# Draining a projection from two PSUM banks instead of four, with the square and the column sums cut in halves

## The chip, the cores and the metric

The kernel runs on one Trainium2 chip, the same program on all 8 cores. Each core has two of the 16 sequences, and no core waits for another. The time is device microseconds of the slowest core: 2117.3 us as the median of 9 runs (2113.49 to 2324.63). The profile is of one execution on core 0.

Four engines matter here. TensorE (PE) multiplies and writes to PSUM, eight banks of 128x512 float32, called `pb[0]` to `pb[7]`. VectorE (DVE) does the element-wise work and reads the banks. ScalarE (ACT) does Ln, Exp and ReLU. DMA queues move the weights and the tiles; GpSimd (POOL) and SyncE (SP) only issue DMAs. Each engine runs its own instructions in program order, and engines wait for each other by counting semaphores: `s_T` counts what PE has done, `s_V` DVE, `s_S` ACT.

## The reference

One layer on x of 16 sequences x 2048 positions x 1024 features:

```
x = x + attn(layernorm(x))      # attn is a linear recurrence (a scan), not softmax
x = x + ffn(layernorm(x))

attn(x): delta = 0.99*sigmoid(x @ W_t.T + b_t) + 0.01
         Bu    = x @ W_b.T + b_b                    # 16 states
         h     = scan over positions: h = exp(A*delta)*h + Bu
         y     = (h @ W_c.T + b_c) + x * D
         return y @ W_o.T + b_o                     # 1024 x 1024
ffn(x):  h = bitlinear(x, w_fc) + gate*(x @ v.T @ fast_b.T @ u.T)    # 1024 -> 4096
         return bitlinear(relu(h)**2, w_proj)                        # 4096 -> 1024
layernorm(x) = (x - mean) / sqrt(mean(x*x) - mean**2 + 1e-5)
bitlinear rounds a weight matrix to -1, 0, 1 times a scale.
```

## The kernel before

Features lie on partitions and positions on the free axis. A tile is 512 positions x 1024 features, held as 8 column blocks of 128 features (`DCH = 8`); a core has 8 tiles, j = 0 to 7. A first stage of some 400 us rounds the weights and writes them to scratch memory. Then the tiles go through a pipeline written out by hand:

```
    for i in range(nt):
        emit_ffnA(i)
        rs1 = emit_front1(i + 2) if i + 2 < nt else None
        emit_ffnB(i)
        if i + 1 < nt:
            s2 = emit_back1(i + 1)
        if i + 2 < nt:
            emit_front1b(i + 2, rs1, ffb_last[i])
        if i + 1 < nt:
            emit_back2(i + 1, s2)
        if i + 2 < nt:
            emit_front2(i + 2)
```

Each `emit_` call appends instructions to the engines' queues in this order, so the order of the calls is the order on every engine. Tile 0 goes through `front1`, `front1b`, `front2`, `back1` and `back2` ahead of the loop, and tile 1 through the three front parts.

- `emit_ffnA` (L898): 256 matmuls in 32 groups of 8 that alternate between banks 2 and 3; ACT drains each group with a ReLU (L919) and DVE squares the result (L929).
- `emit_front1` (L552 to L605): square, cast and column sums of the tile two ahead, and its layer-norm statistics.
- `emit_ffnB` (L954): 256 matmuls, alternating between banks 6 and 7; DVE adds each group to the residual (L972).
- `emit_back1` (L723 to L801): the recurrence's output (L723 and L748), then the 1024 x 1024 projection with W_o, called `_wo` here: 64 matmuls (L768), 8 for each of 8 column blocks. Block `oc` goes to bank `2 + oc % 4`. DVE drains four blocks after the fourth is done, adding the bias `bo_s` and the input `x_s` (L782, in `_wo_stt`); PE may start the second four after all four banks are drained. After the eighth drain DVE squares the whole tile (L799) and casts it to bf16 (L801).
- `emit_front1b` (L619 to L632): the first layer norm of the tile two ahead, on DVE: two groups of 8 instructions that write `tls` and `xnb`.
- `emit_back2` (L812 to L877): the second layer norm. `_stats2` on PE sums the columns of the cast (L812, bank 0) and of the square (L815, bank 1) by 8 matmuls each with a matrix of ones; DVE reads the sums at L823 and L825, ACT does Ln and Exp, and DVE writes the normalised tile (L867, L877).
- `emit_front2` (L645 to L706): the projection to 2 x 16 rows and the scan, with DVE and ACT handing over to each other (L656 to L706).

The next `emit_ffnA` needs the tile of `emit_back2` and, since ACT works in order, its ReLUs stand behind the Exp of `emit_front2` (L691).

Of the kernel before, what the change touches and what calls it, by code (L numbers as in the profile page):

```python
# [26 lines left out]
def build_nc(spc=SEQ_PER_CORE, tps=TILES_PER_SEQ, h=H):  # L27
# [483 lines left out]
    def _gx2(g):  # L511
# [22 lines left out]
    ffa_last = {}  # L534
    sq_chunks = {}
    ffb_last = {}
    run = {"statsv1": 0, "wo_stt": 0, "final": 0, "yb": 0, "tmp2": 0,
           "tls": 0, "nz": 0, "relu": 0}
# [171 lines left out]
    def emit_back1(j):  # L710
# [48 lines left out]

        def _wo(te, j=j, V1=V1):  # L760
            wait(te, "tensor", "s_V", yb_done[j])
            wait(te, "tensor", "s_S", run["relu"])
            for oc in range(DCH):
                b = 2 + oc % 4
                if oc >= 4:
                    wait(te, "tensor", "s_V", V1 + 1)
# [6 lines left out]

        def _wo_stt(ve, j=j):
            if j >= 2:
                wait(ve, "vector", "s_out%d" % (j % 2), 16 * ((j - 2) // 2 + 1))
            for g in range(2):
                wait(ve, "vector", "s_T", wod[4 * g + 3])
                last = None
                for q in range(4):  # L780
                    oc = 4 * g + q
                    last = ve.scalar_tensor_tensor(out=xn32[:, p, oc], in0=pb[2 + oc % 4][:],  # L782
                                                   scalar=bo_s[:, oc:oc + 1],
                                                   in1=x_s[:, p, oc],
                                                   op0=ALU.add, op1=ALU.add)
                inc(last, "s_V")
# [10 lines left out]
        def _sqln2(ve, j=j, ws=ws):  # L797
            wait(ve, "vector", "s_V", ws)
            ve.tensor_tensor(out=xnb[:, p], in0=xn32[:, p], in1=xn32[:, p],  # L799
                             op=ALU.mult)  # L800
            inc(ve.tensor_copy(out=yb[:], in_=xn32[:, p]), "s_V")  # L801
        blk.vector(_sqln2)
        return ctr["s_V"]

    def emit_back2(j, sq2_done):
        p = j % 2

        def _stats2(te, j=j, sq2_done=sq2_done):
            wait(te, "tensor", "s_V", sq2_done)
            wait(te, "tensor", "s_V", yb_done[j])  # L810
            for dc in range(DCH):
                te.matmul(pb[0][:], ones_b[:], yb[:, dc],  # L812
                          start=(dc == 0), stop=(dc == DCH - 1))
            for dc in range(DCH):
                i2 = te.matmul(pb[1][:], ones_b[:], xnb[:, p, dc],  # L815
# [67 lines left out]
    def emit_ffnA(i):  # L883
# [37 lines left out]
        run["relu"] = ctr["s_S"]  # L921
# [181 lines left out]
```

How the kernel before makes its waits and increments, by code:

```python
    def inc(ins, name, k=1):  # L167
        ins.then_inc(sems[name], k)
        ctr[name] += k
        return ctr[name]
# [1 line left out]
    def wait(e, ename, name, val):  # L172
        if val is None or val <= 0:
            return
        key = (ename, name)
        if lastwait.get(key, 0) >= val:
            return
        e.wait_ge(sems[name], val)
        lastwait[key] = val
```

## Time and profile before

| | |
|---|---|
| median of 9 runs | 2117.3 us |
| the profiled execution | 2117.43 us, of which its span is 2115.9 us |
| cores | 2100.4 to 2115.9 us |
| PE busy | 1390.7 us (66%) |
| DVE busy | 891.9 us (42%) |
| ACT busy | 332.5 us (16%) |
| granted TensorE clock, mean over the span | 0.82 of full speed |

No engine is busy all the time. The shares are averages over stages of different kinds: within a tile, PE works almost without a gap in the two feed-forward stages, and between them DVE and ACT work through a long chain while PE mostly waits. So a stage has to be read by its own timeline. A matmul's row is longer (379 ns) than the distance between two of them, because matmuls overlap.

### The profile page before, as it was taken

To read this page: it belongs to the slowest core of one execution; us is meant where nothing else is said; L and a number is where in the kernel's file an instruction comes from. 1 tells how busy PE (TensorE), PEld (TensorE's weight loads), DVE (VectorE), ACT (ScalarE), POOL (GpSimd) and SP (SyncE) were. 2 spreads that over 40 slices of the span, in tenths; PEclk is the share of its full clock that TensorE was granted. 3 is DMA by queue.
4 is the path that set the end of the run, shared out by engine and by line. 5 is a ranking of instruction groups with operands and counts; after the bars stand their busy time and mean duration, and the time that the engine had idled before them with its cause. 6 is when DMAs were issued, how large, how long until landed. Compare 5 with 4: busy or idle time off the path is not lost.

```text
span 2115.9 us, 14743 instructions; the slowest of 8 cores (2100.4 to 2115.9 us)
## 1 busy us (share of the span) xinstructions
PE 1390.7 (66%) x5768; PEld 620.5 (29%) x5768; DVE 891.9 (42%) x925; ACT 332.5 (16%) x392; POOL 27.0 (1%) x42
## 2 busy tenths in 40 slices
PE   1444354324288739874896589568956885798498
PEld 0111154301133314321342234223422332343143
DVE  1777878554612271236214521543164325312410
ACT  1111112010131013002300220032003200310120
POOL 0000000000000000000000000000000000000000
PEclk9766577657699979986998799779978997898799
DMA  6333446421031413241334024312521250234033
GB/s 124 99 119 119 119 139 186 154 97 40 0 120 67 172 40 120 81 158 44 115 106 172 23 97 154 124 43 77 183 96 62 77 214 5 81 118 159 20 120 139
DMA packets 73236, 221.43 MB, mean 105 GB/s; under 512 B 4512, under 2 KB 37280, under 8 KB 54720
## 3 DMA queue, kind: packets, MB, share of 16 engines
q1 hardware_dynamic: 60208, 167.79, 23.4%
q0 software_dynamic: 12960, 52.69, 7.0%
q8 instruction: 47, 0.77, 0.2%
q14 instruction: 21, 0.17, 0.0%
HBM read 189.28 MB, written 33.55 MB: 105 GB/s over the span
## 4 chain that ended last, share of the span: by engine, by line
PE 57%; DVE 28%; issue 6%; ACT 4%; DMA 4%; DVEq 0%; POOL 0%; POOLq 0%; ACTq 0%; SPq 0%
PE pb L954 21%; PE pb L898 20%; PE pb L768 6%; PE pb L357 3%; DVE xn L782 2%; PE pb L442 2%; DVE tls L622 2%; DVE tls L867 2%; DVE xnb L632 2%; DVE xnb L877 2%; DVE cb L383 2%; DVE sqbuf L552 2%; DVE cb L384 2%; DMA woT_b<-woT 2%; DMA wsl<-wprojT 1%
## 5 line engine op out<-in xcount | busy, mean ns | idle before, releaser
L898 PE MATMUL pb<-xnb,wcmb_st 128*128 128x512 bf16 x2048 | 468.5, 393 | 134.8 <-DVE but L658 79.2
L954 PE MATMUL pb<-r2b,wproj_st 128*128 128x512 bf16 x2048 | 444.0, 379 | 0.6 <-DMA wproj_st<-wproj_sc 0.5
L898 PEld LDWEIGHTS pb<-xnb,wcmb_st 128*128 128x128 bf16 x2048 | 205.0, 101 | 398.4 <-issue 174.3
L954 PEld LDWEIGHTS pb<-r2b,wproj_st 128*128 128x128 bf16 x2048 | 199.9, 98 | 243.3 <-issue 3.9
L929 DVE TENSOR_TENSOR r2b<-r2b 128x4096 bf16<-128x4096 bf16 x32 | 73.4, 2292 | 385.3 <-ACT r2b L919 385.3
L972 DVE TENSOR_TENSOR xn<-xn,pb 128x512 f32<-128x512 f32 x64 | 44.0, 688 | 366.3 <-PE pb L954 366.3
L919 ACT ACTIVATE r2b<-pb 128x512 bf16<-128x512 f32 x256 | 152.1, 597 | 286.7 <-PE pb L898 286.6
L768 PE MATMUL pb<-yb,woT_b 128*128 128x512 bf16 x512 | 130.8, 420 | 37.1 <-DVE xn L782 23.8
L844 ACT ACT_TABLE_LOAD x8 | 10.3, 1283 | 762.4 <-DVE statB L838 762.4
L560 PE MATMUL pb<-xb,ones_b 128*128 128x512 bf16 x64 | 28.6, 626 | 125.1 <-DVE xb L553 125.1
L782 DVE SCALAR_TENSOR_TENSOR xn<-pb,bo_s,x_s 128x512 f32<-128x512 f32 x64 | 43.6, 745 | 135.6 <-PE pb L768 135.6
L304 PE MATMUL pb<-GTb,v_b 16*128 16x512 bf16 x64 | 22.1, 450 | 115.3 <-DVE wr L311 115.2
L768 PEld LDWEIGHTS pb<-yb,woT_b 128*128 128x128 bf16 x512 | 53.1, 106 | 118.1 <-issue 71.7
L812 PE MATMUL pb<-yb,ones_b 128*128 128x512 bf16 x64 | 28.2, 619 | 77.7 <-DVE yb L801 77.7
L645 PE MATMUL pb<-xnb,wbtT_b 128*16 128x512 bf16 x64 | 28.6, 626 | 61.5 <-DVE xnb L632 61.5
L442 PE MATMUL pb<-aw32p,ones 128*128 128x128 f32 x256 | 39.7, 332 | 42.3 <-ACT aw32p L434 42.3
L723 PE MATMUL pb<-hbt,wcT_b 16*128 16x512 bf16 x64 | 26.8, 511 | 60.9 <-DVE yb L748 48.8
L442 PEld LDWEIGHTS pb<-aw32p,ones 128*128 128x128 f32 x256 | 39.0, 247 | 43.7 <-issue 43.7
L560 PEld LDWEIGHTS pb<-xb,ones_b 128*128 128x128 bf16 x64 | 8.2, 138 | 141.8 <-issue 141.8
L748 DVE SCALAR_TENSOR_TENSOR yb<-pb,bc_s,tmp 128x512 bf16<-128x512 f32 x64 | 45.1, 746 | 5.5 <-PE pb L723 2.9
L304 PEld LDWEIGHTS pb<-GTb,v_b 16*128 16x128 bf16 x64 | 5.7, 99 | 133.1 <-issue 129.6
L552 DVE TENSOR_TENSOR sqbuf<-x_s 128x4096 bf16<-128x4096 f32 x8 | 35.3, 4418 | 19.6 <-DMA x_s<-xT 19.6
(106 smaller groups left out, 1153.8 us busy)
## 6 DMA issues: line engine op xcount, KB each, us to landing
wcmb_st<-wcmb_sc SPq DMA_DIRECT2D x64, 1024.0 KB, 4.8
wproj_st<-wproj_sc SPq DMA_DIRECT2D x64, 1024.0 KB, 5.0
x_s<-xT POOLq DMA_DIRECT2D x8, 2048.0 KB, 8.4
yT<-xn POOLq DMA_DIRECT2D x8, 2048.0 KB, 9.2
wsl<-wfcT SPq DMA_DIRECT2D x4, 2048.0 KB, 10.3
wslB<-wfcT SPq DMA_DIRECT2D x4, 2048.0 KB, 10.2
wcmb_sc<-wr POOLq DMA_DIRECT2D x8, 1024.0 KB, 4.1
wsl<-wprojT SPq DMA_DIRECT2D x4, 2048.0 KB, 9.7
```

The lines of the kernel that those rows point to most:

```text
L357: i2 = te.matmul(pb[0][:], ones32[:], av[:, dc], start=(dc == 0), stop=(dc == DCH - 1))
L383: ve.tensor_tensor(out=cb1[:], in0=wv[:], in1=hf, op=ALU.is_gt)
L442: i2 = te.matmul(pb[0][:, 0:128], ones32[:], av2[:, kc], start=(kc == 0), stop=(kc == hch - 1))
L552: ve.tensor_tensor(out=sqbuf[:], in0=src, in1=src, op=ALU.mult)
L748: ins = ve.scalar_tensor_tensor(out=yb[:, dc], in0=pb[dc % 2][:], scalar=bc_s[:, dc:dc + 1], in1=tmp2[:, q], op0=ALU.add, op1=ALU.add)
L768: i2 = te.matmul(pb[b][:], woT_b[:, kc, oc * 128:(oc + 1) * 128], yb[:, kc], start=(kc == 0), stop=(kc == DCH - 1))
L782: last = ve.scalar_tensor_tensor(out=xn32[:, p, oc], in0=pb[2 + oc % 4][:], scalar=bo_s[:, oc:oc + 1], in1=x_s[:, p, oc], op0=ALU.add, op1 ...
L898: i2 = te.matmul(pb[b][:], wcmb_st[:, hs % 2, dc, (hc % 4) * 128:(hc % 4 + 1) * 128], xnb[:, p, dc], start=(dc == 0), stop=(dc == DCH - 1))
L919: inc(sc.activation(out=r2b[:, hc], in_=pb[b][:], func=AF.Relu), "s_S")
L929: inc(ve.tensor_tensor(out=r2b[:, qq * QS:(qq + 1) * QS], in0=r2b[:, qq * QS:(qq + 1) * QS], in1=r2b[:, qq * QS:(qq + 1) * QS], op=ALU.mul ...
L954: i2 = te.matmul(pb[b][:], wproj_st[:, oc % 2, kc, :], r2b[:, kc], start=(kc == 0), stop=(kc == hch - 1))
L972: inc(ve.tensor_tensor(out=xn32[:, p, oc], in0=xn32[:, p, oc], in1=pb[b][:], op=ALU.add), "s_V")
```

## The change

`_wo` now uses two banks, 4 and 5, alternating by block, and each drain signals for itself: PE may start block `oc` as soon as block `oc - 2` is drained. DVE waits for each block by itself and drains it at once. The numbers in `STTN` are the counts of `s_V`: the fifth count is the first half of the square, so that blocks 4 to 7 have the counts 6 to 9. The wait of `_wo` for the ReLUs (`run["relu"]`) goes with banks 2 and 3.

The square of the tile is cut in two: the first four blocks are squared right behind the fourth drain, the last four behind the eighth; the cast follows. `_stats2` sums the square first, in two halves with a wait each, and then the cast; it uses banks 7 and 6 in place of 1 and 0. The load of the tile two ahead (`_pref`) waits for the count behind the cast rather than the one behind the last drain.

```diff
@@ emit_back1
+        STTN = [1, 2, 3, 4, 6, 7, 8, 9]
+
         def _wo(te, j=j, V1=V1):
             wait(te, "tensor", "s_V", yb_done[j])
-            wait(te, "tensor", "s_S", run["relu"])
             for oc in range(DCH):
-                b = 2 + oc % 4
-                if oc >= 4:
-                    wait(te, "tensor", "s_V", V1 + 1)
+                b = 4 + oc % 2
+                if oc >= 2:
+                    wait(te, "tensor", "s_V", V1 + STTN[oc - 2])
                 for kc in range(DCH):
                     i2 = te.matmul(pb[b][:], woT_b[:, kc, oc * 128:(oc + 1) * 128],
                                    yb[:, kc], start=(kc == 0), stop=(kc == DCH - 1))
@@ _wo_stt
-            for g in range(2):
-                wait(ve, "vector", "s_T", wod[4 * g + 3])
-                last = None
+            for g2 in range(2):
                 for q in range(4):
-                    oc = 4 * g + q
-                    last = ve.scalar_tensor_tensor(out=xn32[:, p, oc], in0=pb[2 + oc % 4][:],
-                                                   scalar=bo_s[:, oc:oc + 1],
-                                                   in1=x_s[:, p, oc],
-                                                   op0=ALU.add, op1=ALU.add)
-                inc(last, "s_V")
+                    oc = 4 * g2 + q
+                    b = 4 + oc % 2
+                    wait(ve, "vector", "s_T", wod[oc])
+                    inc(ve.scalar_tensor_tensor(out=xn32[:, p, oc], in0=pb[b][:],
+                                                scalar=bo_s[:, oc:oc + 1],
+                                                in1=x_s[:, p, oc],
+                                                op0=ALU.add, op1=ALU.add), "s_V")
+                hw = ctr["s_V"]
+
+                def _sqh(ve2, j=j, g2=g2, hw=hw):
+                    wait(ve2, "vector", "s_V", hw)
+                    sl = slice(4 * g2, 4 * g2 + 4)
+                    inc(ve2.tensor_tensor(out=xnb[:, p, sl], in0=xn32[:, p, sl],
+                                          in1=xn32[:, p, sl], op=ALU.mult), "s_V")
+                _sqh(ve)
+                sqh[g2] = ctr["s_V"]
+            inc(ve.tensor_copy(out=yb[:], in_=xn32[:, p]), "s_V")
+            sqh[2] = ctr["s_V"]
-        def _sqln2(ve, j=j, ws=ws):
-            wait(ve, "vector", "s_V", ws)
-            ve.tensor_tensor(out=xnb[:, p], in0=xn32[:, p], in1=xn32[:, p],
-                             op=ALU.mult)
-            inc(ve.tensor_copy(out=yb[:], in_=xn32[:, p]), "s_V")
-        blk.vector(_sqln2)
@@ emit_back2
-            wait(te, "tensor", "s_V", sq2_done)
-            wait(te, "tensor", "s_V", yb_done[j])
+            wait(te, "tensor", "s_V", back1_sqh[j][0])
+            wait(te, "tensor", "s_V", run["final"])
+            for dc in range(4):
+                te.matmul(pb[7][:], ones_b[:], xnb[:, p, dc],
+                          start=(dc == 0), stop=False)
+            wait(te, "tensor", "s_V", back1_sqh[j][1])
+            for dc in range(4, DCH):
+                te.matmul(pb[7][:], ones_b[:], xnb[:, p, dc],
+                          start=False, stop=(dc == DCH - 1))
+            wait(te, "tensor", "s_V", back1_sqh[j][2])
             for dc in range(DCH):
-                te.matmul(pb[0][:], ones_b[:], yb[:, dc],
-                          start=(dc == 0), stop=(dc == DCH - 1))
-            for dc in range(DCH):
-                i2 = te.matmul(pb[1][:], ones_b[:], xnb[:, p, dc],
+                i2 = te.matmul(pb[6][:], ones_b[:], yb[:, dc],
                                start=(dc == 0), stop=(dc == DCH - 1))
```

The first place is DVE's queue around the drains, for a tile in the loop. In the names, `xn_44` is `xn32`, the residual; `pb` is any bank; `[waits s_T]` says that the instruction waits for PE. Before:

```order
L782 SCALAR_TENSOR_TENSOR xn_44<-pb,bo_s,x_s 128x512 [waits s_T]
L782 SCALAR_TENSOR_TENSOR xn_44<-pb,bo_s,x_s 128x512 x3
L782 SCALAR_TENSOR_TENSOR xn_44<-pb,bo_s,x_s 128x512 [waits s_T]
L782 SCALAR_TENSOR_TENSOR xn_44<-pb,bo_s,x_s 128x512 x3
L802 UNCONDITIONAL_BRANCH
L799 TENSOR_TENSOR xnb<-xn_44 128x4096 [waits s_V]
L801 CAST yb<-xn_44 128x4096
```

The same place of DVE's queue in the changed kernel, whose line numbers differ:

```order
L786 SCALAR_TENSOR_TENSOR xn_44<-pb,bo_s,x_s 128x512 [waits s_T] x4
L795 TENSOR_TENSOR xnb<-xn_44 128x2048 [waits s_V]
L786 SCALAR_TENSOR_TENSOR xn_44<-pb,bo_s,x_s 128x512 [waits s_T] x4
L795 TENSOR_TENSOR xnb<-xn_44 128x2048 [waits s_V]
L799 CAST yb<-xn_44 128x4096
```

Half of the square has moved ahead of the fifth drain, and each drain waits for its own block.

The second place is PE's queue from the projection to the sums, for the first tile; `yb` is first the projection's input and later the cast, `woT_b` the projection's weight, `ones_b` the matrix of ones. Before:

```order
L768 MATMUL pb<-yb,woT_b 128x512 [waits s_V]
L768 MATMUL pb<-yb,woT_b 128x512 x31
L768 MATMUL pb<-yb,woT_b 128x512 [waits s_V]
L768 MATMUL pb<-yb,woT_b 128x512 x31
...
L812 MATMUL pb<-yb,ones_b 128x512 [waits s_V]
L812 MATMUL pb<-yb,ones_b 128x512 x7
L815 MATMUL pb<-xnb,ones_b 128x512 x8
```

The end of the projection (its last block) and the sums in PE's queue of the changed kernel:

```order
L770 MATMUL pb<-yb,woT_b 128x512 [waits s_V]
L770 MATMUL pb<-yb,woT_b 128x512 x7
L832 UNCONDITIONAL_BRANCH
L821 MATMUL pb<-xnb,ones_b 128x512 x4
L825 MATMUL pb<-xnb,ones_b 128x512 [waits s_V]
L825 MATMUL pb<-xnb,ones_b 128x512 x3
L829 MATMUL pb<-yb,ones_b 128x512 [waits s_V]
L829 MATMUL pb<-yb,ones_b 128x512 x7
```

The projection has a wait in front of each block from the third on instead of one in the middle, and the sums of the square have moved ahead of those of the cast, with the only wait for the whole cast in front of the last 8.

## Rows read from the trace of the kernel before

**Rows 1.** The page: span, and shares of the chain that ended last.

```profile
span 2115.9 us, 14743 instructions; the slowest of 8 cores (2100.4 to 2115.9 us)
...
PE 57%; DVE 28%; issue 6%; ACT 4%; DMA 4%; DVEq 0%; POOL 0%; POOLq 0%; ACTq 0%; SPq 0%
```

**Rows 2.** Groups by line: line, engine, shapes, count | busy us, mean ns | idle.

```profile
L768 PE MATMUL pb<-yb,woT_b 128*128 128x512 bf16 x512 | 130.8, 420 | 37.1 <-DVE xn L782 23.8 <-DVE yb L748 13.3
L782 DVE SCALAR_TENSOR_TENSOR xn<-pb,bo_s,x_s 128x512 f32<-128x512 f32 x64 | 43.6, 745 | 135.6 <-PE pb L768 135.6
...
L632 DVE TENSOR_TENSOR xnb<-tls,statA 128x512 bf16<-128x512 f32 x64 | 39.2, 684 | 0.8
...
L799 DVE TENSOR_TENSOR xnb<-xn 128x4096 bf16<-128x4096 f32 x8 | 35.4, 4425 | 0.8
```

**Rows 3.** Waits: who waited for whom: total us, times, longest us.

```profile
PE pb L768 <- DVE xn L782: 23.8, 8, 3.0
...
DVE statB L823 <- PE pb L815: 13.0, 2, 6.6
```

**Rows 4.** Timeline of one tile: start us, us, instruction, count [idle before].

```profile
1108.97 0.90 SPq L987 DMA_DIRECT2D wcmb_st<-wcmb_sc  x2
...
1133.48 9.09 PE L768 MATMUL pb<-yb,woT_b 128*128 128x512 bf16 x32 [1.68 <-DVE yb L748]
1133.86 0.15 PEld L768 LDWEIGHTS pb<-yb,woT_b 128*128 128x128 bf16 x1 [0.27 <-issue]
1134.29 0.15 PEld L768 LDWEIGHTS pb<-yb,woT_b 128*128 128x128 bf16 x1 [0.28 <-issue]
...
1142.68 2.73 DVE L782 SCALAR_TENSOR_TENSOR xn<-pb,bo_s,x_s 128x512 f32<-128x512 f32 x4 [9.45 <-PE pb L768]
...
1145.55 7.07 PE L768 MATMUL pb<-yb,woT_b 128*128 128x512 bf16 x32 [2.98 <-DVE xn L782]
1152.72 2.73 DVE L782 SCALAR_TENSOR_TENSOR xn<-pb,bo_s,x_s 128x512 f32<-128x512 f32 x4 [7.32 <-PE pb L768]
1155.56 4.42 DVE L799 TENSOR_TENSOR xnb<-xn 128x4096 bf16<-128x4096 f32 x1
1156.01 0.88 POOL L793 DMA_DIRECT2D x_s<-xT  x1 [31.06 <-DVE xn L782]
1159.90 2.29 DVE L801 CAST yb<-xn 128x4096 bf16<-128x4096 f32 x1
1162.10 0.68 DVE L619 TENSOR_TENSOR statA<-statA 128x512 f32<-128x512 f32 x1
...
1162.33 3.57 PE L812 MATMUL pb<-yb,ones_b 128*128 128x512 bf16 x8 [9.71 <-DVE yb L801]
...
1172.53 0.68 DVE L823 TENSOR_SCALAR statB<-pb 128x512 f32<-128x512 f32 x1
...
1192.11 5.34 PE L898 MATMUL pb<-xnb,wcmb_st 128*128 128x512 bf16 x16 [12.89 <-DVE but L658]
...
1201.78 1.09 ACT L919 ACTIVATE r2b<-pb 128x512 bf16<-128x512 f32 x2
...
1202.52 12.81 PE L898 MATMUL pb<-xnb,wcmb_st 128*128 128x512 bf16 x51 [5.07 <-ACT r2b L919]
```

**Rows 5.** Windows: stretch, its us, busy us (count) by engine, PEclk, DMA.

```profile
1127.40:1137.60 10.20, 6.13 (x14) 1.73 (x15) 5.27 (x10) 0.00 (x0) 0.00 (x0) 0.50 0.45 186
1137.60:1154.60 17.00, 12.04 (x55) 5.12 (x53) 4.60 (x7) 0.00 (x0) 0.00 (x0) 1.00 0.00 0
...
1202.50:1205.80 3.30, 3.28 (x8) 1.19 (x9) 0.00 (x0) 0.36 (x1) 0.00 (x0) 0.50 0.02 5
1206.00:1256.00 50.00, 50.00 (x233) 22.50 (x230) 6.88 (x3) 17.32 (x29) 0.00 (x0) 1.00 0.35 126
```

**Rows 6.** Timeline of the last tile, around its sums.

```profile
1950.45 8.50 PE L768 MATMUL pb<-yb,woT_b 128*128 128x512 bf16 x32 [2.98 <-DVE xn L782]
...
1968.67 3.57 PE L812 MATMUL pb<-yb,ones_b 128*128 128x512 bf16 x8 [9.71 <-DVE yb L801]
...
1974.95 0.69 DVE L823 TENSOR_SCALAR statB<-pb 128x512 f32<-128x512 f32 x1 [6.42 <-PE pb L815]
```

More of the change, by code:

```diff
@@ L534, in build_nc @@
     ffa_last = {}
+    back1_sqh = {}
     sq_chunks = {}
@@ L537, in build_nc @@
     run = {"statsv1": 0, "wo_stt": 0, "final": 0, "yb": 0, "tmp2": 0,
-           "tls": 0, "nz": 0, "relu": 0}
+           "tls": 0, "nz": 0}
     def emit_front1(j):
@@ L772, in emit_back1 @@
         wo_mm[j] = dict(wod)
+        sqh = {}
         def _wo_stt(ve, j=j):
@@ L795, in emit_back1 @@
             blk.gpsimd(_pref)
-        def _sqln2(ve, j=j, ws=ws):
-            wait(ve, "vector", "s_V", ws)
-            ve.tensor_tensor(out=xnb[:, p], in0=xn32[:, p], in1=xn32[:, p],
-                             op=ALU.mult)
-            inc(ve.tensor_copy(out=yb[:], in_=xn32[:, p]), "s_V")
-        blk.vector(_sqln2)
+        back1_sqh[j] = dict(sqh)
         return ctr["s_V"]
@@ L822, in _sv2 @@
             wait(ve, "vector", "s_T", st)
-            ve.tensor_scalar(out=mB, in0=pb[0][:], scalar1=1.0 / D,
+            ve.tensor_scalar(out=mB, in0=pb[6][:], scalar1=1.0 / D,
                              scalar2=None, op0=ALU.mult)
-            inc(ve.tensor_scalar(out=uB, in0=pb[1][:], scalar1=1.0 / D,
+            inc(ve.tensor_scalar(out=uB, in0=pb[7][:], scalar1=1.0 / D,
                                  scalar2=EPS, op0=ALU.mult, op1=ALU.add), "s_V")
@@ L920, in emit_ffnA @@
         blk.scalar(_relu)
-        run["relu"] = ctr["s_S"]
         QS = max(1, hch // 4)
```

## The prediction

> **What bounds the kernel now.** I read the page first, for the span and the chain that ended last [rows 1]: PE has 57% of the chain and DVE 28%, so stages that PE bounds alternate with stages that DVE bounds, and the shares alone do not say which kind the change touches. The groups by line [rows 2] then give a duration and a count for each instruction concerned: 64 drains of 0.745 us (L782) and 8 squares of 4.425 us (L799) in 8 tiles. The waits [rows 3] name two that the change touches: PE waits 8 times for the drains, 23.8 us in all, and DVE waits twice for the column sums, 13.0 us in all. Last comes the timeline of one tile in the loop [rows 4], where the reader is to follow who waits for whom. PE does 32 matmuls of the projection (1133.48, 9.09 us); DVE drains four blocks (1142.68, 2.73 us) while PE stands still for 2.98 us; PE does 32 more (7.07 us); DVE drains four more, squares (4.42 us), casts (2.29 us) and goes at once into the next layer norm (1162.10). From there to the first ReLU (1201.78) and to the restart of PE's long stage (1202.52) the work is DVE's and ACT's, in a chain in which the drains' end sets the start of everything. So every microsecond by which the cast ends earlier moves the restart by as much, unless something else is late. The weights of the restart are no candidate: their loads were issued at 1108.97, 93 us ahead of it [rows 4].
>
> **Part 1: PE's wait in the middle of the projection.** It is 2.98 us in each of the 8 tiles [rows 3, 4]. With two banks in turn, PE starts block 2 when block 0 is drained. A block is a quarter of 7.07 us, 1.77 us, at the full clock; the way from a block's end through its drain back to PE is 0.11 (1142.57 to 1142.68) + 0.745 + 0.14 (1145.41, the end of the drains, to 1145.55) = 1.0 us [rows 2, 4]. That lies beside the other bank's block, so blocks 2 to 5 start without a wait. Block 6 waits for the drain of block 4, and the half square now stands in front of that drain in DVE's queue. No row has a half square. Two float32 products of two tensors bound it, 0.684 us for 512 columns (L632) and 4.425 us for 4096 [rows 2]: the slope is 3.741 / 3584 = 1.044 ns per column, so 2048 columns take 0.684 + 1536 x 0.001044 = 2.29 us. From the end of block 3: 0.11 + 0.745 + 0.11 + 2.29 + 0.745 + 0.14 = 4.14 us until PE may start block 6. PE has blocks 4 and 5 to do, 3.53 us. So it stands still for 0.6 us. From below the stall is 0 (if DVE's instructions overlap a little more), from above 2.3 us (the half square wholly exposed); I take 0.6, the sum of the rows. Gain of the part: 2.98 - 0.6 = 2.4 us per tile.
>
> **Part 2: the drains after the last block.** Before, four stand there, 2.73 us; now one, 0.745 us, as the other three lie beside PE's blocks. Gain 2.0 us per tile. The waits of each drain for its own block cost nothing: behind them in DVE's queue stands only the rest of the same tile.
>
> **Part 3: the square.** After the last drain 4.42 us become 2.29 us; the first half lies beside PE's blocks 4 and 5, and what it costs there is the stall of part 1. Gain 2.1 us per tile. The cast stays at 2.29 us.
>
> **Part 4: the column sums.** In six tiles the layer norm of another tile stands between the cast and the read of the sums on DVE, from 1162.10 to 1172.53, 10.4 us; PE's 16 sums take less (13.0 us of waiting in 2 tiles is all there is), so their order and banks are worth nothing there [rows 3, 4]. In tiles 0 and 7 nothing stands between, and DVE waits 6.6 and 6.4 us [rows 3, 6]. There 8 of the 16 sums now lie ahead of the end of the cast: four start right behind the projection, four behind the second half square, beside the 2.29 us of the cast. Left are 8. At 1.2 GHz 8 take 3.57 us (L812 [rows 4, 6]), with 0.25 us of handing over 3.8 us; at 2.4 GHz, a quarter of 7.07 us and the same, 2.0 us. PE has worked with shorter pauses before them than before, so either is possible; I take the middle, 2.9 us. Gain 3.6 us in each of two tiles, 7.2 us together (bounds 5.4 and 9.0).
>
> **What costs nothing.** The wait for the ReLUs that goes was never the last one: PE starts the projection on DVE's `yb` (L748), 1.68 us after its own last work [rows 4]. The load of the tile two ahead waits for the cast now; the cast ends where the last drain ended before (1155.5 against 1155.45), so the load is issued at the time it was (1156.01). PE's first four sums wait for counts that the projection has waited for already.
>
> **The sum.** Parts 1 to 3 give 2.4 + 2.0 + 2.1 = 6.5 us in each of 8 tiles, 52 us; part 4 gives 7 us; together 59 us. The profiled execution took 2117.43 us (span 2115.9, 1.5 us around it), which is the median of the runs within 0.2 us: 2117.4 - 59 = 2058.4 us.
>
> **The clock.** TensorE was granted 0.50 (1.2 GHz) until 1137.60, that is for the first ten matmuls of the projection (4.12 us at 0.43 us each), after a stretch in which it had little to do, and 1.00 (2.4 GHz) from there to the end of the second group, over its own pause of 2.98 us too [rows 5]. At 1.2 GHz two weight loads are 0.43 us apart (1133.86, 1134.29), at 2.4 GHz a matmul takes 7.07 / 32 = 0.22 us: 0.21 us for each that changes sides. With shorter pauses I keep the ten at 1.2 GHz and expect the rest at 2.4. After the wait of 5.07 us the restart has 8 matmuls at 1.2 GHz [rows 4, 5]; the stretch ahead of it is the same chain as before, so I keep these 8 too.
>
> A rule of the Trainium skill speaks against this part of the change: "TensorE: Matmul & The Clock Gate", section "A second HAM failure mode: psum-queue depth-cycling", tells of a kernel that goes round its PSUM banks, pauses briefly between groups, and swings between both clocks. By that rule the projection with two banks would lose what rival 3 below loses. This case's trace disagrees as far as it goes: the long stage L898 alternates between two banks as well and was granted 1.00 for 50 us [rows 5].
>
> **Rivals.**
>
> 1. *The gain is partly given back.* Either the half square holds PE up for its whole 2.3 us, 1.7 us more than taken in 8 tiles: 2072 us; or the restart, coming at another moment, has 16 matmuls at 1.2 GHz in place of 8: 8 x 0.21 = 1.7 us in 7 tiles, 2070 us. For it: DVE's queue is strict, and the last tile had a second group of 8.50 us instead of 7.07 [rows 6], so the clock does not fall at the same matmul each time. Against it: PE's wait is the same in all 8 tiles (23.8 us, the longest 3.0 [rows 3]), so the tiles repeat each other closely. Chance 10%.
>
> 2. *More is gained.* If the restart has no matmuls at 1.2 GHz, 7 tiles give another 12 us: 2046 us. Against it: PE still stands for 5 us before it. Chance 6%.
>
> 3. *Slower: two banks keep the projection at 1.2 GHz.* The place is the projection; the price is 64 matmuls at 0.43 us, 27.5 us, against 9.09 + 2.98 + 7.07 = 19.1 us, so 8.4 us more per tile in place of part 1's gain. Parts 2 and 3 still give 4.1, so the tile loses 4.3 us, 8 tiles 34 us, less 7 us of part 4: 2144 us. It decides when the lost matmuls outweigh 6.5 + 0.9 us per tile: 7.4 / 0.21 = 35 more than the ten, 45 of the 64. Against it: one wait of 0.6 us in a stretch that kept the clock over 2.98 us. Chance 2%.
>
> 4. *Nothing moves.* If something other than DVE's chain held the ReLU or the restart, the saved time would stand there as a new wait, and the time stays at 2117 us. I find no such thing in the timeline: the weights are there, and DVE has no idle time in front of L619 or L823 [rows 4]. Chance 2%.
>
> **How the numbers follow.** The forecast, 2058 us, has 80%; its own range, by the bounds of the stall (5 us down) and of the sums and half of a clock effect, is 2051 to 2066. The rivals have 10, 6, 2 and 2%. For 8 in 10 the range reaches somewhat towards rivals 1 and 2: 2047 to 2069. A difference of 0.2% (4 us) is about what a measurement of this kernel can tell from none. Faster takes the forecast and rivals 1 and 2, 96%; the same is rival 4, 2%; slower rival 3, 2%.
>
> **What would show it.** In the changed kernel's timeline the projection is one burst of about 16.8 us with at most one pause, of about 0.6 us, in front of block 6; behind it stand one drain, a square of 2.29 us and the cast; from the projection's start to the cast's end it takes about 22.2 us rather than 28.7. In the list of waits the 23.8 us of PE for the drains fall to about 5, DVE's wait for PE at the drains goes from 16 waits to many short ones, and the two waits for the sums fall from 6.5 to about 3 us. The distance from one tile's projection to the next falls by 6.5 us. Wrong would be: a pause before other blocks (the drains are slower than taken), a projection at clock 0.50 beyond the first dozen matmuls (rival 3), more matmuls at 1.2 GHz at the restart (rival 1), or a new idle time in front of L619 or the first ReLU (rival 4).

## The result, and the profile after

The changed kernel takes 2057.04 us as the median of 10 runs (2053.77 to 2241.16), the kernel before 2118.3 us beside it; the ratio is 0.971, with a 95% interval of 0.9702 to 0.9719. The forecast was 2058, the saving forecast 59 us; measured it is 61. (The highest times come from runs in which one die ran at a lower clock; the ratios leave them out.)

The page of the kernel after, profiled on core 1; it answers to [rows 1].

```profile
span 2057.0 us, 14848 instructions; the slowest of 8 cores (2040.9 to 2057.0 us)
...
PE 57%; DVE 29%; issue 6%; ACT 4%; DMA 4%; DVEq 0%; POOL 0%; POOLq 0%; ACTq 0%; SPq 0%
```

The shares are those of before within one point: 59 us of span went, and the page alone would not tell from where. The groups by line do (busy us, mean ns of one, idle before). L770 is the projection, L786 the drain, L795 the new half square; they answer to [rows 2].

```profile
L770 PE MATMUL pb<-yb,woT_b 128*128 128x512 bf16 x512 | 128.8, 415 | 17.7 <-DVE yb L749 12.9 <-DVE xn L786 4.9
L786 DVE SCALAR_TENSOR_TENSOR xn<-pb,bo_s,x_s 128x512 f32<-128x512 f32 x64 | 47.3, 749 | 75.9 <-PE pb L770 75.9
L795 DVE TENSOR_TENSOR xnb<-xn 128x2048 bf16<-128x2048 f32 x16 | 36.7, 2292 | 1.7
```

A drain costs what it did (749 ns after 745), and two half squares cost 36.7 us in all after 35.4 for the whole ones. So no instruction became cheaper; what fell is waiting. The waits (total us, times, longest us) answer to [rows 3]:

```profile
DVE xn L786 <- PE pb L770: 75.9, 48, 3.8
...
DVE statB L837 <- PE pb L829: 6.7, 2, 3.8
...
PE pb L770 <- DVE xn L786: 4.9, 8, 0.6
```

PE's waits for the drains are still 8, but of 0.6 us instead of 3.0. DVE waits 48 times for a block, 1.6 us each, 75.9 us in all, where it waited for whole groups of four before, 135.6 us in all [rows 2]. The timeline of one tile on core 1 (start us, us, instruction, count [idle before]) answers to [rows 4]:

```profile
1112.62 12.25 PE L770 MATMUL pb<-yb,woT_b 128*128 128x512 bf16 x48 [1.56 <-DVE yb L749]
...
1121.53 0.75 DVE L786 SCALAR_TENSOR_TENSOR xn<-pb,bo_s,x_s 128x512 f32<-128x512 f32 x1 [0.97 <-PE pb L770]
1122.38 2.29 DVE L795 TENSOR_TENSOR xnb<-xn 128x2048 bf16<-128x2048 f32 x1
1124.59 1.40 DVE L786 SCALAR_TENSOR_TENSOR xn<-pb,bo_s,x_s 128x512 f32<-128x512 f32 x2
...
1125.48 3.61 PE L770 MATMUL pb<-yb,woT_b 128*128 128x512 bf16 x16 [0.61 <-DVE xn L786]
...
1129.20 0.75 DVE L786 SCALAR_TENSOR_TENSOR xn<-pb,bo_s,x_s 128x512 f32<-128x512 f32 x1 [0.97 <-PE pb L770]
1130.05 2.29 DVE L795 TENSOR_TENSOR xnb<-xn 128x2048 bf16<-128x2048 f32 x1
1132.26 2.29 DVE L799 CAST yb<-xn 128x4096 bf16<-128x4096 f32 x1
...
1164.48 5.02 PE L912 MATMUL pb<-xnb,wcmb_st 128*128 128x512 bf16 x16 [13.21 <-DVE but L659]
...
1174.89 10.33 PE L912 MATMUL pb<-xnb,wcmb_st 128*128 128x512 bf16 x41 [5.39 <-ACT r2b L933]
```

Six blocks run without a pause, the one pause stands in front of block 6, and behind the last block come one drain, a half square and the cast, which ends at 1134.55: 21.9 us after the projection's start, where it was 28.7. PE's restart at 1174.89 is 62.3 us after that start; in [rows 4] it is 69.0. The 6.8 us by which the cast came earlier arrive whole at the restart. The windows of the same tile (stretch, its us, busy us (count) of PE, PEld, DVE, ACT and POOL, PEclk, DMA) answer to [rows 5]:

```profile
1112.60:1116.30 3.70, 3.68 (x10) 1.32 (x11) 0.00 (x0) 0.00 (x0) 0.00 (x0) 0.52 0.00 0
1116.30:1129.10 12.80, 12.19 (x57) 5.41 (x56) 7.37 (x8) 0.00 (x0) 0.00 (x0) 1.00 0.00 0
1174.80:1178.20 3.40, 3.31 (x10) 1.29 (x11) 0.00 (x0) 0.44 (x2) 0.00 (x0) 0.59 0.00 0
1178.40:1228.40 50.00, 49.77 (x231) 22.37 (x229) 6.88 (x3) 17.24 (x30) 0.00 (x0) 1.00 0.35 126
```

Again some ten matmuls at the start of the projection are at 1.2 GHz, the rest at 2.4, over the pause of 0.61 us too; and at the restart again about 3 us are at 1.2 GHz.

### The profile page after: what moved, and what is told of

Read it like the earlier page. It is cut to its first block, busy times and chain, and to the rows that moved or that the text cites. A ratio compares the mean times of both kernels' runs of the same rounds, so it can differ in the third digit from the quotient of the medians.

```text
span 2057.0 us, 14848 instructions; the slowest of 8 cores (2040.9 to 2057.0 us)
## 1 busy us (share of the span) xinstructions
PE 1375.6 (67%) x5768; PEld 614.2 (30%) x5768; DVE 896.1 (44%) x933; ACT 332.6 (16%) x392; POOL 26.9 (1%) x42
## 4 chain that ended last, share of the span: by engine, by line
PE 57%; DVE 29%; issue 6%; ACT 4%; DMA 4%; DVEq 0%; POOL 0%; POOLq 0%; ACTq 0%; SPq 0%
PE pb L912 21%; PE pb L967 21%; PE pb L770 5%; PE pb L357 3%; PE pb L442 2%; DVE tls L881 2%; DVE tls L623 2%; DVE xnb L633 2%; DVE xnb L891 2%; DVE cb L383 2%; DVE sqbuf L553 2%; DVE cb L384 2%; DMA woT_b<-woT 2%; DVE cb L471 2%; DVE cb L472 1%
## 5 line engine op out<-in xcount | busy, mean ns | idle before, releaser
L912 PE MATMUL pb<-xnb,wcmb_st 128*128 128x512 bf16 x2048 | 466.9, 392 | 137.8 <-DVE but L659 81.5
L912 PEld LDWEIGHTS pb<-xnb,wcmb_st 128*128 128x128 bf16 x2048 | 204.5, 100 | 400.2 <-issue 175.4
L770 PE MATMUL pb<-yb,woT_b 128*128 128x512 bf16 x512 | 128.8, 415 | 17.7 <-DVE yb L749 12.9
L770 PEld LDWEIGHTS pb<-yb,woT_b 128*128 128x128 bf16 x512 | 52.6, 105 | 97.2 <-issue 49.8
L786 DVE SCALAR_TENSOR_TENSOR xn<-pb,bo_s,x_s 128x512 f32<-128x512 f32 x64 | 47.3, 749 | 75.9 <-PE pb L770 75.9
L442 PE MATMUL pb<-aw32p,ones 128*128 128x128 f32 x256 | 39.7, 332 | 46.1 <-DVE dbuf L478 18.6
```

The lines of the kernel that those rows point to most:

```text
L442: i2 = te.matmul(pb[0][:, 0:128], ones32[:], av2[:, kc], start=(kc == 0), stop=(kc == hch - 1))
L770: i2 = te.matmul(pb[b][:], woT_b[:, kc, oc * 128:(oc + 1) * 128], yb[:, kc], start=(kc == 0), stop=(kc == DCH - 1))
L786: inc(ve.scalar_tensor_tensor(out=xn32[:, p, oc], in0=pb[b][:], scalar=bo_s[:, oc:oc + 1], in1=x_s[:, p, oc], op0=ALU.add, op1=ALU.add), " ...
L912: i2 = te.matmul(pb[b][:], wcmb_st[:, hs % 2, dc, (hc % 4) * 128:(hc % 4 + 1) * 128], xnb[:, p, dc], start=(dc == 0), stop=(dc == DCH - 1))
```

## The experiments

Three theories were held against each other; the expectations name them by letters. A: the saving is a sum of microseconds on the chain from the projection through DVE to PE's restart, as predicted. B: the same, but what reaches the time depends on how many matmuls run at 1.2 GHz after it. C: the saving is TensorE's clock, which shorter pauses keep up.

To hold the kernels against each other, this table has the means over the five inner tiles (1 to 5) of all 8 cores (40 distances), read out of the traces: from a projection's start to the end of the cast and to PE's restart (us), the us at granted clock 0.50 within the projection and behind the restart, and the distance from one projection's start to the next.

```
kernel       cast end  restart  1.2 GHz: projection  restart   distance
before         28.62    68.95            3.96         3.27      204.83
x1_drains      23.80    64.21            4.55         5.20      201.27
x2_halves      27.78    68.12            6.53         4.97      204.75
x3_sums        28.59    68.93            3.90         3.24      204.77
after          22.15    62.48            3.97         3.26      198.10
x4_fourbanks   21.43    61.77            4.08         3.41      197.99
x5_quarters    20.51    60.99            4.37         4.82      197.93
x7_tail1       22.75    63.15            3.96         5.24      199.66
x7_tail4       24.46    64.87            4.19         3.99      201.38
x8_front4      22.25    62.66            4.03         3.64      198.42
x10_fill       22.02    62.39            3.82         0.00      196.32
x6_ahead       20.34    55.14            4.03         3.38      191.23
x12_allfill    18.71    53.53            0.70         0.00      185.48
```

### The parts one by one

**Drains and banks alone** (x1_drains), on the kernel before; the square stays whole, the sums stay behind the cast.

```diff
-                b = 2 + oc % 4
-                if oc >= 4:
-                    wait(te, "tensor", "s_V", V1 + 1)
+                b = 4 + oc % 2
+                if oc >= 2:
+                    wait(te, "tensor", "s_V", V1 + oc - 1)
...
-            for g in range(2):
-                wait(ve, "vector", "s_T", wod[4 * g + 3])
+            for oc in range(DCH):
+                wait(ve, "vector", "s_T", wod[oc])
```

> The kernel before with two banks and a drain of its own for each block; the square stays whole and the sums stay as they were. Theory A (each part is worth what it takes off the path from the projection's start to the cast's end): 2.98 us of PE's wait and 2.0 us of drains go in each of 8 tiles, and no half square stands in front of block 4's drain, so 5.0 x 8 = 40 us: 2078 us against 2118. Theory C (the gain is TensorE's clock, since the projection has no pause any more): nearly all of the 60 us, 2060 us.

Measured: 2081.83 us, ratio 0.9826 [0.9812, 0.9839]. The groups of this kernel show that PE's pause for the drains is gone; only the wait for `yb` is left:

```profile
L767 PE MATMUL pb<-yb,woT_b 128*128 128x512 bf16 x512 | 128.8, 418 | 12.5 <-DVE yb L748 12.5
```

That is 38 us less than the kernel before beside it (2119.65). By C the whole gain, some 60 us, should have been here: C falls. The cast ends 4.8 us earlier, close to A's 5.0 (the pause of 2.98 and three drains), but the distance of the tiles falls by 3.6 only: behind the restart 5.20 us are at 1.2 GHz instead of 3.27.

**The square in halves alone** (x2_halves), on the kernel before, with four banks and drains in fours.

```diff
+                wait(ve, "vector", "s_V", ctr["s_V"])
+                sl = slice(4 * g, 4 * g + 4)
+                inc(ve.tensor_tensor(out=xnb[:, p, sl], in0=xn32[:, p, sl],
+                                     in1=xn32[:, p, sl], op=ALU.mult), "s_V")
...
-            ve.tensor_tensor(out=xnb[:, p], in0=xn32[:, p], in1=xn32[:, p],
-                             op=ALU.mult)
```

> The kernel before with its four banks and its drains in fours, with the square alone cut in two halves, one behind each four drains. Theory A: 4.42 - 2.29 = 2.1 us in each of 8 tiles, 17 us: 2101 us, and PE's wait of 2.98 us stays. Theory B (TensorE's clock takes back part of a small gain at the restart of the long stage, as more matmuls at 1.2 GHz): 8 to 14 us, 2104 to 2110 us. Theory C: no change, 2118 us.

Measured: 2113.93 us, ratio 0.9972 [0.9962, 0.9981]: 6 us where the sum asks for 17. The windows of core 4 over two successive projections show why; the first four rows are one projection, the last two the next (PEclk is the third number from the end).

```profile
926.60:931.20 4.60, 4.54 (x11) 1.61 (x12) 0.00 (x0) 0.00 (x0) 0.00 (x0) 0.50 0.02 4
931.30:938.00 6.70, 4.68 (x22) 1.93 (x20) 1.91 (x3) 0.00 (x0) 0.00 (x0) 1.00 0.00 0
938.10:944.90 6.80, 5.94 (x15) 2.05 (x16) 3.01 (x3) 0.00 (x0) 0.00 (x0) 0.50 0.00 0
945.00:949.00 4.00, 3.96 (x19) 1.58 (x17) 0.00 (x0) 0.00 (x0) 0.00 (x0) 1.00 0.00 0
1132.90:1136.00 3.10, 3.03 (x8) 1.10 (x9) 0.00 (x0) 0.00 (x0) 0.00 (x0) 0.50 0.00 0
1136.10:1151.70 15.60, 12.52 (x58) 5.32 (x55) 5.02 (x5) 0.00 (x0) 0.00 (x0) 1.00 0.00 0
```

In the first projection the clock came up, fell at 938.1 in PE's pause of 2.98 us, and came up once more: 15 more matmuls ran at 1.2 GHz. In the next one it stayed up over the same pause. On this core long projections (22.2 us, 11.4 of them at 1.2 GHz) and short ones (18.6 us) alternate tile by tile. Behind the last block the half square saves 2.1 us, as A has it; the clock takes it back in the projection (6.53 us at 1.2 GHz instead of 3.96) and at the restart (4.97 instead of 3.27). That is B's side, and more of it than B had expected. What decides which projection is long stays open.

**The sums alone** (x3_sums), on the kernel before: PE takes the columns' sums of the square, which is there first, ahead of those of the cast.

```diff
+            wait(te, "tensor", "s_V", sq_only[j])
+            for dc in range(DCH):
+                te.matmul(pb[1][:], ones_b[:], xnb[:, p, dc],
+                          start=(dc == 0), stop=(dc == DCH - 1))
             wait(te, "tensor", "s_V", sq2_done)
-            wait(te, "tensor", "s_V", yb_done[j])
             for dc in range(DCH):
-                te.matmul(pb[0][:], ones_b[:], yb[:, dc],
-                          start=(dc == 0), stop=(dc == DCH - 1))
-            for dc in range(DCH):
-                i2 = te.matmul(pb[1][:], ones_b[:], xnb[:, p, dc],
+                i2 = te.matmul(pb[0][:], ones_b[:], yb[:, dc],
...
```

> The kernel before with one thing changed: the column sums take the square first, behind a wait for the square alone, and the cast after it. Theory A: only tiles 0 and 7 see it, where 8 of the 16 sums now lie beside the 2.3 us of the cast; they run at 1.2 GHz (3.4 us for 8), so 2.0 to 2.3 us are hidden in each: the two waits for the sums fall from 6.5 to 4.3 us, the time by 4 us, 2114 us against 2118. That the sums matter in the other tiles: 8 x 2 = 16 us.

Measured: 2110.56 us, ratio 0.997 [0.9958, 0.9983], so 0.3%, 6 to 7 us. Its waits give 5.7 us of that in the first and the last tile, 13.0 us before and now

```profile
DVE statB L824 <- PE pb L816: 7.3, 2, 3.7
```

and nothing in the tiles between (distance 204.77 after 204.83). A had 4 us. In the first and the last tile this order alone brings nearly all of what the whole change brings there (13.0 to 6.7 us). The three edits alone give 38 + 6 + 7 = 51 us, the whole change gives 61: the parts don't add up. Both that lie in the inner tiles gave part of their saving back to the clock, and the whole change did not.

### Two banks or four, and a finer split

**Four banks** (x4_fourbanks), on the kernel after: PE waits for the drain four blocks back, and for the ReLUs again.

```diff
-                b = 4 + oc % 2
-                if oc >= 2:
-                    wait(te, "tensor", "s_V", V1 + STTN[oc - 2])
+                b = 2 + oc % 4
+                if oc >= 4:
+                    wait(te, "tensor", "s_V", V1 + STTN[oc - 4])
...
```

> The changed kernel with four banks in turn (2 to 5) instead of two, all else as changed: block 6 waits for block 2's drain, so the half square no longer holds PE up. Theory A: the pause of 0.61 us goes in 8 tiles, 5 us: 2052 us against 2057. Theory B: the projection ends 0.6 us earlier, but the distance from tile to tile stays at 198.0 us, since the restart has more matmuls at 1.2 GHz: 2056 to 2057 us. That two banks as such matter: slower or faster than 2057 by more than 5 us.

Measured: 2057.54 us, ratio 0.9705 [0.969, 0.972]: the same. The pause of 0.6 us is gone and the cast ends 0.7 us earlier, but the tiles follow at 197.99 us. Of the 0.7 us, 0.1 go in 0.15 us more at 1.2 GHz behind the restart, and 0.4 in the 16 column sums of `emit_front1`, between the two long stages: 5.18 us of them are at 1.2 GHz in place of 4.45 (means of the same 40 tiles), and a microsecond at 1.2 GHz does half of what it does at 2.4. B had 2056 to 2057 us, for the restart alone. So the two banks were not the cost, and the stall of part 1 was not worth removing.

**The square in quarters** (x5_quarters), on the kernel after, each quarter behind two drains; 6 sums stand ahead of the last quarter.

```diff
-            for g2 in range(2):
-                for q in range(4):
-                    oc = 4 * g2 + q
+            for g2 in range(4):
+                for q in range(2):
+                    oc = 2 * g2 + q
...
```

> The changed kernel with the square in quarters, one behind every second drain. A quarter takes 0.684 + 512 x 0.001044 = 1.22 us. Theory A: behind the last drain 1.22 us instead of 2.29, and no pause in front of block 6: 1.07 + 0.61 = 1.7 us in 8 tiles, 13 us: 2044 us against 2057. Theory B: the distance from tile to tile stays at 198.0 us and only tile 0 and the stretch behind the last projection gain: 3 us, 2054 us.

Measured: 2052.32 us, ratio 0.9688 [0.9673, 0.9704]. Timeline of one tile on core 2, the last quarter, the cast and the restart; then the windows of that restart:

```profile
926.96 1.23 DVE L795 TENSOR_TENSOR xnb<-xn 128x1024 bf16<-128x1024 f32 x1
928.10 2.29 DVE L799 CAST yb<-xn 128x4096 bf16<-128x4096 f32 x1
...
971.08 4.42 PE L912 MATMUL pb<-xnb,wcmb_st 128*128 128x512 bf16 x10 [4.49 <-ACT r2b L933]
```

```profile
971.00:975.65 4.65, 4.57 (x11) 1.61 (x12) 0.00 (x0) 1.02 (x2) 0.00 (x0) 0.50 0.00 0
975.80:1010.00 34.20, 34.20 (x161) 15.48 (x159) 4.58 (x2) 11.54 (x20) 0.00 (x0) 1.00 0.43 154
```

A quarter takes 1.23 us, and the cast ends 20.5 us after the start, 1.6 earlier, as A has it. Then the restart stays at 1.2 GHz for 4.6 us (mean 4.82, after 3.26), and the tiles follow at 197.93 us. Of the 13 us that A saw in the 8 tiles 5 arrive, hardly any of them in the inner tiles (0.17 us each). The restart comes 1.5 us earlier; 0.8 of that goes behind the restart and 0.6 in the 16 column sums of `emit_front1` (5.57 us at 1.2 GHz in place of 4.45). B was nearer.

### Cost put in at the same place

**A square of 512 columns in front of the cast** (x7_tail1), on the kernel after; it writes to a buffer that nobody reads then.

```diff
+            ve.tensor_tensor(out=xb[:, 0:1], in0=xn32[:, p, 0:1],
+                             in1=xn32[:, p, 0:1], op=ALU.mult)
```

> The changed kernel with one DVE instruction more per tile, ahead of the cast: it squares 512 columns into a buffer that nobody reads at that time. Theory A (each us on the way from the drains to the cast's end is a us of the tile): 0.62 to 0.68 us in 8 tiles, 5 us: 2062 us against 2057. Theory B (the tile distance holds at a value, and TensorE's matmuls at 1.2 GHz make up the difference): the distance stays 198.0 us in the loop, only tile 0 and the stretch behind the last projection pay: 2058 us.

Measured: 2069.38 us, ratio 0.9794 [0.9753, 0.9834] (wide, as one of the times compared was 2090). The cast ends 0.60 us later, and 8 x 0.6 would make 5 us; it cost 12. Windows of core 3, the restarts of two successive tiles, each with the stretch behind it:

```profile
978.95:981.65 2.70, 2.68 (x7) 1.00 (x8) 0.00 (x0) 0.36 (x1) 0.00 (x0) 0.51 0.00 0
981.80:1000.00 18.20, 18.20 (x86) 8.29 (x85) 2.29 (x1) 6.46 (x11) 0.00 (x0) 1.00 0.37 126
1177.55:1183.10 5.55, 5.50 (x14) 1.95 (x15) 0.00 (x0) 0.99 (x2) 0.00 (x0) 0.51 0.00 0
1183.20:1200.00 16.80, 16.80 (x80) 7.64 (x78) 2.29 (x1) 5.88 (x10) 0.00 (x0) 1.00 0.34 127
```

Seven matmuls at 1.2 GHz in the one tile, fourteen in the other. The first of the two tiles is 198.57 us long, 0.5 more than the mean of the kernel after, as A has it; the other is 201.01. A (2062) and B (2058, the cost swallowed) were both too low: the clock did decide, but against this edit.

**The same with 2048 columns** (x7_tail4), 2.28 us.

```diff
+            ve.tensor_tensor(out=xb[:, 0:4], in0=xn32[:, p, 0:4],
+                             in1=xn32[:, p, 0:4], op=ALU.mult)
```

> The same with 2048 columns, 2.2 to 2.3 us per tile, as long as the half square that the change takes off this place. Theory A: 18 us, 2075 us, and the distance from tile to tile is 200.2 us. Theory B: the distance jumps from 198.0 to the next value seen so far, 201.3 us, as in the kernel with two banks alone: about 25 us, 2082 us.

Measured: 2081.78 us, ratio 0.9831 [0.9818, 0.9845]: 24 us more than the kernel of the next run, for 8 x 2.3 = 18. The cast ends 2.31 us later and the distance grows by 3.28, with 3.99 us at 1.2 GHz behind the restart in place of 3.26, and 5.13 in the column sums of `emit_front1` in place of 4.45. B had 2082. On cores 0 and 1 the long stage also has stretches at a third granted clock, here on core 0:

```profile
1396.85:1401.52 4.67, 4.67 (x20) 1.96 (x18) 2.29 (x1) 1.19 (x2) 0.00 (x0) 0.81 0.51 172
```

They are not what the edit cost: on core 5, which has none, the distance grows as much (198.00 to 201.36).

**The same square in front of the first drain** (x8_front4), where DVE waits for PE anyway: the same work, at another place.

```diff
+            ve.tensor_tensor(out=xb[:, 0:4], in0=x_s[:, p, 0:4],
+                             in1=x_s[:, p, 0:4], op=ALU.mult)
```

> The changed kernel with the same 2.3 us of DVE work per tile, put in front of the first drain, where DVE waits 3.8 us for PE's first block. Theories A and B: it is hidden, 2057 us. That DVE's busy time as such counts: 18 us, 2075 us.

Measured: 2058.05 us, ratio 0.9721 [0.9708, 0.9735]: free. Timeline of DVE on core 0:

```profile
910.04 2.28 DVE L781 TENSOR_TENSOR xb<-x_s 128x2048 bf16<-128x2048 f32 x1
913.95 0.75 DVE L788 SCALAR_TENSOR_TENSOR xn<-pb,bo_s,x_s 128x512 f32<-128x512 f32 x1 [1.63 <-PE pb L770]
```

DVE still waits 1.63 us behind it. So 2.3 us of DVE in each tile cost 24 us behind the last drain and nothing ahead of the first: the place decides, not the busy time. That is what makes parts 2 and 3 of the prediction a gain at all, since they only move DVE's work from the one place to the other.

### The clock by itself

**Twenty idle matmuls in front of the restart** (x10_fill), on the kernel after: PE does them while it waits for the first ReLU, into a bank that is not read.

```diff
+                if hc == 2 and i + 1 < nt:
+                    for _ in range(20):
+                        te.matmul(pb[0][:], ones_b[:], xnb[:, p, 0], start=True, stop=True)
```

> The changed kernel with 20 idle matmuls (into bank 0, which nobody reads then) behind the first 16 of the long stage, in the 5.4 us in which PE waits for the first ReLU; 20 take 4.3 us at 2.4 GHz. They are to keep TensorE's clock up, so that the restart has no matmuls at 1.2 GHz. Theory A: the 3.0 us at 1.2 GHz at the restart become 1.5, 7 tiles: 10 us, 2046 us. Theory B: the restart can no longer make up differences, and the distance falls to another value below 198.0, by more than the 1.5 us: up to 24 us, 2033 us. If the fillers run at 1.2 GHz they take 8.5 us and hold the restart up by 3 us: 2078 us.

Measured: 2047.95 us, ratio 0.9673 [0.9659, 0.9686]. Timeline of PE on core 1, and the window of the restart:

```profile
967.82 4.48 PE L910 MATMUL pb<-xnb,ones_b 128*128 128x512 bf16 x20
973.46 26.71 PE L915 MATMUL pb<-xnb,wcmb_st 128*128 128x512 bf16 x123 [1.16 <-ACT r2b L936]
```

```profile
973.40:1000.00 26.60, 26.54 (x123) 12.04 (x124) 3.70 (x2) 9.15 (x16) 0.00 (x0) 1.00 0.36 126
```

The restart comes at the same moment (62.39 after 62.48 us), but at 2.4 GHz from its first matmul. The 3.26 us at 1.2 GHz become 0, half of that is 1.6 us, and the tile is 1.8 us shorter; 9 us in all, near A's 2046. Nothing was computed faster ahead of it: this is the clock alone, and it is what the tested change left untouched.

**DVE's free time used** (x6_ahead). A version that takes the first half of the next tile's layer norm (nine DVE instructions) into DVE's wait ahead of the first drain, with four banks and the square in quarters:

```diff
+        md = ahead() if ahead else None
...
-            emit_front1b(i + 2, rs1, ffb_last[i])
+            emit_front1b_s(i + 2, md)
```

> The kernel with the square in quarters, with four banks for the projection, and with the first half of the next layer norm (9 instructions, 5.4 us of DVE) moved from behind the cast to the time in which DVE waits for PE's first blocks. Theory A: 5.4 us in the six tiles that have a next layer norm there, 32 us off 2052: 2020 us. Theory B (the matmuls at 1.2 GHz change with the restart's moment): the tile distance falls from 198 to a value between 191 and 195, 2010 to 2032 us.

Measured: 2011.43 us, ratio 0.9499 [0.9484, 0.9513]. DVE on core 1, between the end of `yb` and the drains:

```profile
1285.33 1.41 DVE L752 SCALAR_TENSOR_TENSOR yb<-pb,bc_s,tmp 128x512 bf16<-128x512 f32 x2 [0.17 <-PE pb L727]
1286.66 0.68 DVE L620 TENSOR_TENSOR statA<-statA 128x512 f32<-128x512 f32 x1
1287.26 4.90 DVE L623 TENSOR_TENSOR tls<-x_s,statA 128x512 f32<-128x512 f32 x8
1292.07 1.40 DVE L791 SCALAR_TENSOR_TENSOR xn<-pb,bo_s,x_s 128x512 f32<-128x512 f32 x2
```

The place that was free in x8_front4 is used for work that stood on the chain: the restart comes 5.85 us earlier than with the quarters alone (in two banks), where A had 5.4, and the tile is 6.70 us shorter, since the restart also has 1.44 us less at 1.2 GHz; that is why it came out below A's 2020. The first drains are late now (two in a row at 1292.07), and the cast ends no later for it.

**And idle matmuls in four places** (x12_allfill) of that version: 20 at the restart, 40 ahead of a tile's first sums, and 27 around the small matmuls ahead of the projection.

```diff
+                if dc >= 2 and dc % 2 == 0 and j >= 1:
+                    for _ in range((10, 7, 5)[dc // 2 - 1]):
+                        te.matmul(pb[5][:], ones_b[:], woT_b[:, 0, 0:TT], start=True, stop=True)
...
+            for _ in range(5 if j >= 1 else 0):
+                te.matmul(pb[5][:], ones_b[:], woT_b[:, 0, 0:TT], start=True, stop=True)
```

> The kernel x6 with idle matmuls in four places where PE waits in each tile: 20 in front of the restart, 40 in front of the first layer norm's sums, and 10, 7, 5 and 5 between the small matmuls ahead of the projection (into banks that nobody reads then). They are to keep TensorE at 2.4 GHz. By the trace before: 3.4 us at 1.2 GHz at the restart, about 4.8 in the sums and 4.1 in the projection become half, so 1.7 x 7 + 2.4 x 6 + 2.1 x 7 = 41 us off x6, about 1980 us, and the tiles' distances then follow the sum of the parts. If fillers run at 1.2 GHz they delay the work behind them and x12 is slower than x6.

Measured: 1976.56 us, ratio 0.934 [0.9325, 0.9355], the shortest of all; the sum had asked for 1980. Windows of core 4, one whole projection and the restart behind it:

```profile
1454.55:1468.65 14.10, 13.92 (x64) 6.40 (x67) 13.53 (x19) 0.00 (x0) 0.00 (x0) 1.00 0.00 1
1507.65:1540.00 32.35, 32.13 (x147) 14.72 (x151) 4.59 (x2) 11.15 (x19) 0.00 (x0) 1.00 0.37 131
```

The projection is at 2.4 GHz from its first matmul, 14 us instead of 16, though not in every tile: the mean still has 0.70 us at 1.2 GHz.

## Why the prediction was right, point by point

**Part 1, the pause.** Said: 0.6 us, in front of block 6 alone. It is 0.61 us, there and nowhere else, 8 times. Said of the half square, by interpolation between two shapes: 2.29 us; it is 2.292. Removing the rest of the pause brings nothing (x4).

**Part 2, the drains.** Said: one of 0.745 us behind the last block. One of 0.75 stands there. The drains by themselves (x1) brought the cast's end forward by 4.8 us, and a quarter of it was lost again on the way to the next tile.

**Part 3, the square.** Said: 2.1 us. One half square of 2.29 us stands behind the last drain now. Alone the edit gives 0.8 us at the cast's end and 0.1 in the distance (x2), but in the whole change the sum of the three parts closes: 22.15 us from the projection's start to the cast's end as a mean (said: 22.2), and 6.73 us less from tile to tile (said: 6.5).

**Part 4, the sums.** The one term that was mis-sized. Said: 2.9 us of waiting are left, bounds 2.0 and 3.8. It is 3.83 us in tile 0 and 2.87 in tile 7. Timeline of tile 0 on core 1:

```profile
510.21 3.57 PE L829 MATMUL pb<-yb,ones_b 128*128 128x512 bf16 x8 [0.87 <-DVE yb L799]
...
513.89 0.69 DVE L837 TENSOR_SCALAR statB<-pb 128x512 f32<-128x512 f32 x1 [3.83 <-PE pb L829]
```

The eight last sums ran at 1.2 GHz here, 0.45 us each: the upper bound. In tile 7 they took 2.66 us, as the clock came up among them, which is the middle that was taken. So 6.3 us instead of 7.

**What costs nothing.** The load of the tile two ahead is issued at 1135.11, 0.6 us behind the cast, and nothing waits for it; no new wait stands in front of the layer norm or of the first ReLU. Rival 4 falls.

**The clock.** Said: ten matmuls at 1.2 GHz at the projection's start and 8 at the restart, as before. The means say 3.97 and 3.26 us after 3.96 and 3.27. For this change that was true, and so the sum came out. As a rule it is not: x1 and x2 against before, and x5 and x7_tail1 against after, have 1.6 to 2.0 us more at 1.2 GHz behind the restart, and x7_tail4 has 0.7 more. That is what rival 1 had named (16 matmuls in place of 8, 2070 us, 10%). The mean hides that it happened in the changed kernel too: 4 of its 40 tiles have 5.8 to 6.0 us there, the others 2.7 to 3.4. One of the 4, on core 2:

```profile
1171.80:1177.80 6.00, 5.77 (x14) 2.08 (x16) 0.00 (x0) 0.95 (x2) 0.00 (x0) 0.50 0.01 3
```

It cost nothing: against the same tile of core 0 the long stage L912 takes 1.45 us more, but the restart comes 0.45 us earlier and the 16 column sums behind the stage take 0.96 us less, so that both tiles are 198.0 us long. The profile before gave no reason why this change should keep its shares and those five kernels should not, so the step was right here and its ground was not shown; that the forecast missed by one microsecond only is partly luck.

How the pieces add up can be checked on the table. At 1.2 GHz a matmul takes 0.43 us and at 2.4 GHz 0.216, so a microsecond at 1.2 GHz loses half a microsecond. For x7_tail1 against after: the restart 0.67 later, 1.98 us more at 1.2 GHz, 0.99, together 1.66; the distance grew by 1.56. For x1 against before: 4.74 earlier, 0.97 lost, together 3.8; measured 3.56. For x10: 0.09 and 1.63, together 1.72; measured 1.78. What is left (up to 0.3 us; 0.5 in x4, x5 and x7_tail4) is for the most part the clock at a third place, the 16 column sums of `emit_front1`: of these 4.45 us are at 1.2 GHz in the kernel after, and 5.18, 5.57 and 5.13 us in those three. Half of the difference is 0.3 to 0.6 us, and with it the sum closes within 0.3 us in each kernel of the table.

**Rival 3 and its rule.** In the trace two banks with a pause of 0.61 us kept 1.00 for 12.8 us, and four banks without the pause gave the same time (2057.54). The projections that did fall back to 1.2 GHz had four banks and a pause of 2.98 us: 21 of 64 in x2 (8 tiles on 8 cores), 4 in the kernel before and 2 in x3, the last six all in a core's last tile. One of these is the second group of 8.50 us in [rows 6], so the prediction's word that this stretch kept the clock over 2.98 us holds for the tiles in the loop and not for the last one. The Trainium skill, "TensorE: Matmul & The Clock Gate", section "A second HAM failure mode: psum-queue depth-cycling", has the clock swing where a kernel cycles its banks with brief pauses. Here two banks with the brief pause did not do it in any of the 64 projections of the kernel after, and four banks with the long one did in some tiles of three kernels. A brief pause with four banks was not run.

## What to carry to other kernels

Find the instruction whose end starts the next chain, and count only what stands between it and the last result it needs: the same 2.3 us of DVE work in each tile cost 24 us there and nothing in front of the first drain. Sum up such microseconds by rows, then look at what PE does next: a few microseconds at 1.2 GHz behind each long wait can swallow a gain of 1.6 us or turn a cost of 0.6 into 1.6, so a saving that looks certain per tile is certain only up to there. Idle matmuls in PE's waits took that share out; in the last version they were worth 35 us of 2011, more than any finer split.

## What the runs showed of the hardware that was not expected

- How many matmuls run at 1.2 GHz behind a wait is not fixed by the wait. With 0.60 us more of DVE work, the restart took 2.70 us at 1.2 GHz in one tile and 5.55 in the next (x7_tail1), behind the same chain; in the changed kernel it was 3.0 us on core 0 and 6.0 on core 2 in the same tile.
- Tiles with a long and a short projection alternate on one core, 22.2 and 18.6 us, with distances of 206.3 and 203.4 us (x2); what carries this from tile to tile is open.
- Three kernels whose casts end at 20.5, 21.4 and 22.2 us follow tile on tile at 197.9, 198.0 and 198.1 us (x5, x4, after); what the earlier cast gains goes in matmuls at 1.2 GHz at the restart and in the column sums of `emit_front1`.
- In the long stages of all 8 cores of the changed kernel PE was granted 1.00 behind the first microseconds, for 50 us at a time, some 0.216 us for a matmul of 512 columns (231 in 50 us).
- One profile has a third granted clock, 0.81: in x7_tail4 cores 0 and 1 have it for 26 us each, in stretches of 3.7 to 4.7 us, cores 2 and 3 for 3.9 us. The other cores and the other 12 profiles do not have it; what brings it is open.
